# Banks dealt out over the uses that exist, and a new order of tasks on all engines, in a two-layer transformer kernel

## Chip, cores, metric

The kernel runs on one core of one Trainium2 chip. The metric is the device time of one launch in microseconds; lower is better. The whole input of 16 sequences is one launch.

## What is computed

Each of 16 sequences has 512 tokens of 128 features (float32). Two layers follow one another, and in each the attention and the feed-forward network both read the same normalised input and are added to the residual:

```python
xn = _layernorm(x)
x = x + _L0_attn_ref(xn, ...) + _L0_ffn_ref(xn, ...)
xn = _layernorm(x)
x = x + _L1_attn_ref(xn, ...) + _L1_ffn_ref(xn, ...)
```

Layer 0's attention has 16 heads of 64 features, a causal mask and a distance penalty per head. Layer 1's is a differential attention without a mask: 8 heads, each with two softmaxes over 8-feature queries and keys with rotary positions; the second result, times a learned factor, is taken from the first, and each head is normalised before the output projection. Each feed-forward network normalises once more, widens to 512, applies silu and narrows to 128.

## The kernel before

**Sequences and ticks.** Every engine runs a program written out in full, without a loop on the chip. Time is counted in ticks, of which each sequence has a clock of its own. A new sequence starts every 32 ticks (`TICKS`), so that in the middle one period of 32 ticks holds layer 0 of one sequence and most of layer 1 of the one before. Constants such as `FA_AT = 11` or `WOB_AT = 44` (lines 96 to 139) give the tick, on the sequence's clock, at which a task is issued; a tick from 32 on falls in the next period (44 is tick 12 there), a negative one in the period before. `pipeline` (line 563) calls each engine's `body(b)` for b from -1 to 17, and a body goes through ticks 0 to 31. An engine takes its work strictly in this order; engines meet only at semaphores.

**Layer 0** takes two heads (a pair) every four ticks; r is the tick's place in the four. For a pair TensorE projects q and k (r = 0) and v (r = 2), computes scores (`max_scores0`, line 1380: rows 0 and 1 of 128 queries at r = 0, row 2 at r = 1, row 3 at r = 3). VectorE adds the mask and takes the row maximum (`row_max0`), ScalarE exponentiates (`exp0`), VectorE inverts the sums (`invert_sums`), GpSimd scales (`scale_probs`), TensorE transposes in three groups (`turn_probs`, line 1399), ScalarE copies them (`copy_turned`) and TensorE multiplies by v (`pv0`). The output projection comes in two halves, woA and woB (`attention_out`, line 1428). Hidden tiles ya0 to ya3 (layer 1: yb0 to yb3) and the second product fa (fb) are the feed-forward network.

**Layer 1** runs in 46 steps over 28 ticks from tick 58 (`l1_chunk`, line 152), one or two steps in a tick, called its part 0 and part 1. A step has two score tiles for row maxima (`mx1`, steps 0 to 31), and from step 14 on two tiles of transposed scores (`st1`) that ScalarE exponentiates; every second step has a product with the values (`pv1`, line 1442). Both row and key tiles are issued by `second_scores` (line 1469), small transposes by `second_turns` (line 1457), everything that comes once in a sequence by `others`. Queries and keys are rotated on VectorE (`rotate`, line 1104), stored in parts by SyncE's queue (`store_parts`, line 609) and loaded back into the operands QS and KS (`stack`, line 622).

**PSUM banks.** Two banks, `pj`, take all projections and products (63 uses a period); five, `sc`, take score tiles and transposes (224 a period); one, `op`, the layer-1 values. A use's bank is its place in a list of all tasks of a period, modulo two or five: `pj_order` and `score_order` (lines 205 and 243) write that list, and `pj_use` and `tile_before` (lines 339 and 353) tell which use had the bank before, so what an engine must wait for. The place counts all tasks of a full period, also in the first and last periods, where many of them do not run:

```python
def tile_bank(kind, m):

    return TILE_AT[kind, m] % SCB
```

TensorE waits before it writes a bank (`bank`, line 1314, and `bank_free`, line 1369) until VectorE or ScalarE has read the use before.

**Order within a tick.** It is written by hand in each engine's `body`: TensorE's from line 1555, VectorE's from line 1252, ScalarE's from line 931, GpSimd's from line 744, SyncE's from line 641. The tables in the section on the change give it.

## Time and profile before

| what | value |
|---|---|
| time before, median of 3 runs | 2718.11 us (2716.66 to 2722.74) |
| profiled execution, its own time | 2727.31 us |
| its span, first to last instruction | 2725.5 us |
| TensorE busy | 2468.1 us |
| ScalarE / VectorE busy | 1896.9 / 1869.4 us |
| GpSimd busy | 1411.5 us |
| mean granted TensorE clock | 0.982 |

All parts of the prediction rest on one profiled execution, with times in us from the start of its span. TensorE's row of matmuls counts an instruction as busy to a modelled end, so neighbours overlap a little; an idle time in brackets names the instruction on another engine that ended it. A full period is 162.3 us long and repeats to 0.1 us: the input of the next sequence is fetched every 162.30 us.

### The profile page before, as it was taken

How to read it: one execution, taken by the hardware profiler on the slowest of the kernel's cores; microseconds unless marked ns; L12 is line 12 of the kernel's file. 1: busy time of each engine (PE TensorE's matmuls, PEld its weight loads, DVE VectorE, ACT ScalarE, POOL GpSimd, SP SyncE). 2: the span in 40 equal slices, each digit the busy share in tenths (PEclk: the TensorE clock that was granted, in tenths of full speed). 3: DMA queues.
4: the chain of work that ended last, by engine and by line, in shares of the span. 5: the costliest groups of instructions: out<-in, count | busy, mean ns of one | idle time of the engine just before them, and what ended most of it. 6: DMA issues, size and time to landing. Idle time of an engine off the chain costs nothing.

```text
span 2725.5 us, 52475 instructions
## 1 busy us (share of the span) xinstructions
PE 2468.1 (91%) x18176; PEld 1232.3 (45%) x18176; DVE 1869.4 (69%) x5637; ACT 1896.9 (70%) x4707; POOL 1411.5 (52%) x1353
## 2 busy tenths in 40 slices
PE   6899999999999999999999999999999999999877
PEld 3454444454444445444444444445444444544421
DVE  4447677776767767677676867777676776866665
ACT  3766786767777776776767678677777777677435
POOL 4666465554646455464554547455464645546111
PEclk8999999999999999999999999999999999999978
DMA  2002020110202001020200202001020200202020
GB/s 88 5 5 48 5 52 2 31 26 6 51 6 47 5 16 41 6 52 2 49 9 5 52 5 52 2 22 35 6 51 2 52 5 6 51 2 51 2 51 5
DMA packets 59830, 68.57 MB, mean 25 GB/s; under 512 B 11056, under 2 KB 55344, under 8 KB 56368
## 3 DMA queue, kind: packets, MB, share of 16 engines
q1 hardware_dynamic: 59568, 65.21, 10.0%
q8 instruction: 148, 2.42, 0.4%
q14 instruction: 114, 0.93, 0.1%
HBM read 35.04 MB, written 29.36 MB: 24 GB/s over the span
## 4 chain that ended last, share of the span: by engine, by line
PE 65%; DVE 14%; ACT 9%; issue 3%; DMA 0%; SPq 0%; POOLq 0%; DVEq 0%; ACTq 0%; POOL 0%
PE pj L1332 16%; PE sc L1394 10%; PE pj L1424 9%; PE op L1448 8%; PE sc L1492 5%; DVE pq L1095 5%; PE pj L1350 4%; PE pj L1438 4%; ACT pt L885 4%; PE sc L1411 4%; PE sc L1485 3%; DVE mx L1148 2%; PE pj L1324 2%; ACT pt L863 1%; ACT pq L845 1%
## 5 line engine op out<-in xcount | busy, mean ns | idle before, releaser
L713 POOL TENSOR_SCALAR pq<-pq,rsum 128x128 f32<-128x128 f32 (+3 forms) x1024 | 1113.3, 1103 | 1071.3 <-DVE rsum L1102 1071.3
L1148 DVE TENSOR_REDUCE mx<-sc 128x1 f32<-128x512 f32 x1024 | 653.3, 684 | 334.3 <-PE sc L1492 331.3
L885 ACT ACTIVATE pt<-sc 128x512 f32<-128x512 f32 x1024 | 558.4, 608 | 220.2 <-PE sc L1485 219.7
L1095 DVE CUSTOM_DVE_ANT_0 pq<-sc,relkey 128x128 f32<-128x128 f32 (+3 forms) x1024 | 459.0, 486 | 315.5 <-PE sc L1394 308.3
L845 ACT ACTIVATE pq<-pq,mx 128x128 f32<-128x128 f32 (+3 forms) x1024 | 568.0, 568 | 48.6 <-DVE mx L1095 47.3
L863 ACT ACTIVATE pt<-sc 128x512 f32<-128x512 f32 (+1 forms) x768 | 353.8, 530 | 186.9 <-PE sc L1411 185.9
L1394 PE MATMUL sc<-K,Q 64*128 64x128 f32 (+3 forms) x2048 | 383.0, 471 | 25.0 <-ACT pt L885 11.2
L1424 PE MATMUL pj<-pt,v 128*64 128x512 f32 (+3 forms) x2048 | 305.2, 440 | 14.4 <-ACT y L813 8.8
L1332 PE MATMUL pj<-xnT,wqkv 128*128 128x512 f32 x512 | 288.6, 656 | 11.2 <-DVE xb L1069 6.2
L1411 PE MATMUL sc<-ident,pq 64*128 64x64 f32 x5120 | 233.6, 228 | 69.0 <-DVE mx L1095 58.4
L1448 PE MATMUL op<-pt,v 128*32 128x512 f32 x2048 | 279.2, 618 | 13.3 <-ACT pt L885 12.9
L1492 PE MATMUL sc<-KS,QS 48*128 48x512 bf16 x1024 | 243.7, 387 | 47.5 <-DVE mx L1095 20.4
L1411 PEld LDWEIGHTS sc<-ident,pq 64*128 64x128 f32 x5120 | 201.0, 140 | 177.4 <-issue 134.2
L1394 PEld LDWEIGHTS sc<-K,Q 64*128 64x128 f32 x2048 | 147.0, 187 | 252.3 <-issue 158.2
L1485 PE MATMUL sc<-QS,KS 51*128 51x512 bf16 x1024 | 217.2, 387 | 15.8 <-ACT pt L885 10.2
L1424 PEld LDWEIGHTS pj<-pt,v 128*64 128x64 f32 x2048 | 143.0, 137 | 180.0 <-issue 147.8
L845 ACT ACTIVATION_READ_ACCUMULATOR pq<-pq,mx 128x1 f32 x1024 | 210.7, 206 | 0.0
L1485 PEld LDWEIGHTS sc<-QS,KS 51*128 51x128 bf16 x1024 | 54.7, 94 | 222.3 <-issue 134.0
L1492 PEld LDWEIGHTS sc<-KS,QS 48*128 48x128 bf16 x1024 | 60.8, 94 | 196.3 <-DVE mx L1095 64.7
L1332 PE MATMUL pj<-wqkv,xnT 128*128 128x128 f32 x1024 | 147.4, 287 | 1.1 <-DVE K L1076 0.8
L1332 PEld LDWEIGHTS pj<-wqkv,xnT 128*128 128x128 f32 x1024 | 125.8, 193 | 39.7 <-issue 25.7
L811 ACT ACTIVATE tanh<-pj,b1h 128x512 f32<-128x512 f32 x128 | 88.3, 690 | 75.4 <-PE pj L1332 70.4
(105 smaller groups left out, 2822.6 us busy)
## 6 DMA issues: line engine op xcount, KB each, us to landing
scr_p<-y SPq DMA_DIRECT2D x160, 128.0 KB, 2.9
QS<-scr_p SPq DMA_DIRECT2D x32, 384.0 KB, 5.6
KS<-scr_p SPq DMA_DIRECT2D x32, 384.0 KB, 5.6
x_in<-in_L_attn_x SPq DMA_DIRECT2D x16, 256.0 KB, 2.8
scr_p<-tanh SPq DMA_DIRECT2D x32, 128.0 KB, 2.5
out_x<-xres SPq DMA_DIRECT2D x16, 256.0 KB, 2.3
QS<-nrow SPq DMA_DIRECT2D x192, 4.0 KB
wqkv<-in_L_attn_w_qkv SPq DMA_DIRECT2D x1, 1536.0 KB, 6.5
```

The source lines that it names most:

```text
L713: pool.tensor_scalar(rows, rows, rsum[:, p % NROWS, c:c + 1], None, ALU.mult).then_inc(s_scl, 1)
L845: act.activation(rows, rows, ACT.Exp, scale=-1.0, bias=mx0[:, p % NROWS, c:c + 1], accum_out=lsum[:, p % NROWS, c:c + 1]).then_inc(s_exp0, 1)
L863: act.activation(to[:, :, h, :], sc[tile_bank("tr0", m)][:, 0:cols].rearrange("p (n c) -> p n c", c=HALF), ACT.Copy).then_inc(s_ev, 1)
L885: act.activation(pt1[:, GS * (m % 2) + 2 * j + h, :], sc[tile_bank("st1", 2 * n + h)][:, :], ACT.Exp, scale=float(DS) ** -0.25).then_inc(s ...
L1095: dve.tensor_tensor_reduce(out=pq[:, at:at + width], in0=sc[tile_bank("mx0", m)][:, left:left + width], in1=relkey[:, T - width:T], scale= ...
L1148: dve.reduce_max(mx1[:, g % 2, at:at + 1], sc[tile_bank("mx1", 2 * t + h)][:, :], AXIS.X).then_inc(s_mxd1, 1)
L1332: last = pe.matmul(t[:, c * k:c * (k + 1)], w(k), x(k), start=True, stop=True)
L1394: last = pe.matmul(sc[tile_bank("mx0", m + j)][:, left:left + width], Q0[r, b, P * row:P * (row + 1)], K0[r, b, 0:width], start=True, stop ...
L1411: last = pe.transpose(sc[tile_bank("tr0", m + h)][:, HALF * n:HALF * (n + 1)], pq[r, at:at + P], ident[r, r])
L1424: last = pe.matmul(t[DH * j:DH * (j + 1), P * k:T], v0[:, p % NBUF, k, DH * j:DH * (j + 1)], pt[:, base:base + WIDTH[k]], start=k == 0, st ...
L1448: last = pe.matmul(op[32 * j:32 * (j + 1), :], v1[:, k, (GS * g + j) // 2, :], pt1[:, GS * (k % 2) + j, :], start=k == 0, stop=k == NT - 1)
L1492: pe.matmul(sc[tile_bank("mx1", 2 * t + h)][:, :], QS[r, slot, P * q:P * (q + 1)], KS[r, slot, :], start=True, stop=True).then_inc(s_mxf1, 1)
```

## The change

Three things, on all engines together.

1. The lists of bank uses are made over the whole program. `pj_order` and `score_order` now go through all ticks of all sequences, hold only the tasks that run, and `in_turn` deals the banks out one after the other, anew at each period. `tile_before` and `pj_use` look the use up. The two clocks g and h (for tasks of the first and of the second layer) are equal in every tick here, since `CLOCKS` has one entry.
2. Ticks of single tasks move, as the first part of the diff shows; `SCALE_LAG` and `NORM_LAG` move two steps of the head normalisation back in steps of layer 1. `second_scores` is split into `second_keys` (st1) and `second_tops` (mx1), always called in this order.
3. The order within a tick changes. "L1 rows", "L1 scores", "L1 values", "L1" stand for the layer-1 parts; 0 and 1 is the part; "turn 1" is the second group of probability transposes; scores 0, 2, 3 and maxima are by row group:

| engine, r | before | after |
|---|---|---|
| TensorE 0 | q, scores L1 0, k, scores 0, values 0, turn 1, turn 2, rows 0 1, others, values 1, scores L1 1 | q, scores L1 0, rows 0, k, scores 0, turn 1, values 0 1, others, turn 2, rows 1, scores L1 1 |
| TensorE 1 | rows 0, pv, scores L1 0 1, others, values 0, rows 1, scores 2, values 1 | rows 0, pv, scores L1 0, values 0, others, scores L1 1, rows 1, scores 2, values 1 |
| TensorE 2 | scores L1 0, rows 0, v, scores L1 1, others, rows 1, values 0 1 | rows 0, scores L1 0, v, scores L1 1, values 0, others, rows 1, scores 3, values 1 |
| TensorE 3 | rows 0, scores 3, rows 1, scores L1 0, others, values 0, turn 0, values 1, scores L1 1 | rows 0 1, scores L1 0, values 0, others, turn 0, values 1, scores L1 1 |
| VectorE 0 | others, L1 0, maxima 0, norms, copy K, maxima 1, L1 1, invert 2 | invert 1, others, invert 2, L1 0, norms, copy K, maxima 0, maxima 1, L1 1 |
| VectorE 1 | invert 3, L1 0, others, L1 1, norms | invert 3, norms, L1 0 1, others |
| VectorE 2 | norms, others, invert 0, maxima 2, L1 0 1 | maxima 2, norms, others, L1 0, invert 0, L1 1 |
| VectorE 3 | norms, others, maxima 3, L1 0 1, invert 1 | norms, maxima 3, L1 0, others, L1 1 |
| ScalarE 0 | copy Q, L1 0, exp 3, exp 0, others, copy turned 2 3 4, L1 1 | L1 0, exp 3, copy Q, copy turned 2 3, others, copy turned 4 5, L1 1, exp 0 |
| ScalarE 1 | copy turned 5, L1 0, copy attention, others, L1 1, exp 1 | L1 0, others, copy attention, L1 1 |
| ScalarE 2 | L1 0, others, copy v, L1 1 | L1 0, exp 1, L1 1, copy v, others |
| ScalarE 3 | exp 2, others, L1 0, copy turned 0 1, L1 1 | exp 2, L1 0, others, copy turned 0 1, L1 1 |
| GpSimd | r 1: scale 2, small, scale 3; r 2: scale 0, small; r 3: small, scale 1 | r 0: scale 1, small; r 2: scale 2 3 0, small; r 1 and 3: small |

SyncE's queue keeps its order in a tick; the constants move both fills (`STACK_AT`) behind both stores (`STORE_AT`). The diff, cut to the constants, the numbering and TensorE's first tick of four:

```diff
@@ -93,47 +93,48 @@
-X_AT = -18
-LN0_AT = (-14, -9, -1)
+X_AT = -19
+LN0_AT = (-15, -8, -1)
 XNT0_AT = -5
 HT0_AT = -1
-FFN0_AT = (1, 2, 5, 5)
+FFN0_AT = (1, 2, 6, 7)
 FA_AT = 11
 WOA_AT = 35
-WOB_AT = 44
-LN1_AT = (45, 48, 54)
+WOB_AT = 45
+LN1_AT = (47, 48, 54)
 XNT1_AT = 49
 ROPE_AT = (51, 52)
-STORE_AT = (47, 50)
-STACK_AT = (47, 50)
-VALS_AT = 55
+STORE_AT = (49, 50)
+STACK_AT = (54, 54)
+VALS_AT = 54
 HT1_AT = 55
 L1_AT = 58
 L1_TICKS = 28
-FFN1_AT = (56, 56, 57, 59)
+FFN1_AT = (56, 56, 59, 60)
 FB_AT = 62
 TAIL_AT = 86
-TURN3_AT = 86
-OT_AT = 89
-OUT_AT = 90
-HID0_AT = (3, 6, 7, 11)
-HID1_AT = (57, 58, 59, 60)
-ADDA_AT = 12
-ADDB_AT = 63
-ADDWA_AT = 36
+TURN3_AT = 87
+OT_AT = 90
+OUT_AT = 91
+HID0_AT = (2, 5, 7, 10)
+HID1_AT = (57, 59, 60, 61)
+ADDA_AT = 11
+ADDB_AT = 64
+ADDWA_AT = 35
 ADDWB_AT = 45
 TURN_ROPE_AT = (52, 53)
 HEAD3A_AT = 87
-HEAD3B_AT = 90
+HEAD3B_AT = 89
 ADDOUT_AT = 91
-PLN0_AT = (-11, -5)
-PLN1_AT = (48, 49)
-RES0_AT = 3
-RES1_AT = 51
+PLN0_AT = (-9, -7)
+PLN1_AT = (47, 48)
+RES0_AT = 0
+RES1_AT = 53
 HEAD3P_AT = 87
-STOREOUT_AT = 84
+STOREOUT_AT = 89
+CLOCKS = (TICKS * NB,)
...
-SCALE_LAG = 0
-NORM_LAG = 4
+SCALE_LAG = 3
+NORM_LAG = 5
...
+def clocks():
+
+    shown = [(n, n) for n in range(-TICKS, CLOCKS[0])]
+    g = h = CLOCKS[0]
+    for first, second in CLOCKS[1:]:
+        for n in range(max(first, second)):
+            shown.append((g + n if n < first else None, h + n if n < second else None))
+        g, h = g + first, h + second
+    end = TICKS * (NB + 2)
+    while h < end:
+        shown.append((g if g < end else None, h))
+        g, h = g + 1, h + 1
+    return shown
 
 
...
+def in_turn(order, banks):
+
+
+    uses, of_bank, n = {}, [[] for _ in range(banks)], 0
+    for use in order:
+        if use is None:
+            n = 0
+            continue
+        of_bank[n % banks].append(use)
+        uses[use] = (n % banks, len(of_bank[n % banks]))
+        n += 1
+    return uses, of_bank
+
+
 PJ_ORDER = pj_order()
-PJ_AT = {name: n for n, (name, _) in enumerate(PJ_ORDER)}
-PJ_PER = [len(PJ_ORDER[b::2]) for b in range(2)]
-TILES = score_order()
-TILE_AT = {(kind, m): n for n, (kind, _, m) in enumerate(TILES)}
...
+PJ_USES, _ = in_turn(PJ_ORDER, 2)
+TILES, TILES_OF = in_turn(score_order(), SCB)
...
 def tile_before(seq, kind, m):
 
-    n = TILE_AT[kind, m]
-    body = seq.ago(-TILES[n][1])
-    while body.lo >= -1:
-        n -= SCB
-        if n < 0:
-            body = body.ago(1)
-            n = n % SCB + SCB * ((len(TILES) - 1 - n % SCB) // SCB)
-        kind, ago, m = TILES[n]
-        if body.ago(ago).live():
-            return kind, body.ago(ago), m
-    return None
+    bank, n = TILES[kind, m, seq.lo]
+    if n == 1:
+        return None
+    kind, m, lo = TILES_OF[bank][n - 2]
+    return kind, Seq(lo), m
...
-            def body(b):
-
-                used.clear()
-                for n in range(TICKS):
-                    s, r = divmod(n, 4)
-                    if r == 0:
-                        p, i = b.pair(s, -1)
-                        if i is not None:
-                            project_q(i, p)
-                        second_scores(b, n, 0)
-                        p, i = b.pair(s, -1)
-                        if i is not None:
-                            project_k(i, p)
-                        p, i = b.pair(s, 0)
-                        if i is not None:
-                            max_scores0(i, p, 0)
-                        second_values(b, n, 0)
-                        p, i = b.pair(s, 2)
-                        if i is not None:
-                            turn_probs(i, p, 1)
-                        p, i = b.pair(s, 2)
-                        if i is not None:
-                            turn_probs(i, p, 2)
-                        second_turns(b, n, 0)
-                        second_turns(b, n, 1)
-                        others(b, n)
-                        second_values(b, n, 1)
-                        second_scores(b, n, 1)
...
+            def tick(g, h):
+
+                r = (h if g is None else g) % 4
+                if r == 0:
+                    p, i = pair(g, -1)
+                    if i is not None:
+                        project_q(i, p)
+                    second_keys(h, 0)
+                    second_tops(h, 0)
+                    second_turns(h, 0)
+                    p, i = pair(g, -1)
+                    if i is not None:
+                        project_k(i, p)
+                    p, i = pair(g, 0)
+                    if i is not None:
+                        max_scores0(i, p, 0)
+                    p, i = pair(g, 2)
+                    if i is not None:
+                        turn_probs(i, p, 1)
+                    second_values(h, 0)
+                    second_values(h, 1)
+                    others(g, h)
+                    p, i = pair(g, 2)
+                    if i is not None:
+                        turn_probs(i, p, 2)
+                    second_turns(h, 1)
+                    second_keys(h, 1)
+                    second_tops(h, 1)
...
+            pipeline(tick)
+            assert used == [use for use in PJ_ORDER if use is not None]
```

## Rows read from the trace of the kernel before

**Rows 1.** The page, parts 1 and 5: busy time by engine, and one group.

```profile
PE 2468.1 (91%) x18176; PEld 1232.3 (45%) x18176; DVE 1869.4 (69%) x5637; ACT 1896.9 (70%) x4707; POOL 1411.5 (52%) x1353
...
L1148 DVE TENSOR_REDUCE mx<-sc 128x1 f32<-128x512 f32 x1024 | 653.3, 684 | 334.3 <-PE sc L1492 331.3
```

**Rows 2.** Stretches: length, busy us (instructions) by engine, granted clock, DMA share, GB/s.

```profile
71.00:178.00 107.00, 94.07 (x753) 55.12 (x753) 44.90 (x201) 76.81 (x211) 73.74 (x70) 0.97 0.01 4
178.00:326.00 148.00, 135.42 (x1005) 71.13 (x1004) 102.08 (x317) 101.25 (x259) 80.42 (x77) 0.99 0.11 25
...
703.00:865.30 162.30, 150.93 (x1139) 75.90 (x1137) 116.51 (x352) 118.10 (x295) 87.78 (x85) 1.00 0.10 24
...
2654.00:2692.00 38.00, 31.30 (x147) 6.26 (x146) 27.81 (x53) 20.52 (x41) 1.83 (x2) 0.76 0.01 2
```

**Rows 3.** Timeline, TensorE, one period: start, length, line, operation, wait before.

```profile
705.85 0.66 PE L1324 MATMUL pj<-ident,oraw 128*128 128x128 f32 x4 [0.72 <-ACT oraw L869]
...
713.44 0.47 PE L1411 MATMUL sc<-ident,pq 64*128 64x64 f32 x8 [0.44 <-DVE mx L1095]
...
716.41 2.37 PE L1424 MATMUL pj<-pt,v 128*64 128x512 f32 x16 [0.59 <-ACT y L813]
...
720.97 0.38 PE L1492 MATMUL sc<-KS,QS 48*128 48x512 bf16 x2
...
745.88 1.12 PE L1332 MATMUL pj<-xnT,wqkv 128*128 128x512 f32 x2
...
748.80 0.46 PE L1411 MATMUL sc<-ident,pq 64*128 64x64 f32 x8 [0.44 <-DVE mx L1095]
...
776.57 1.12 PE L1332 MATMUL pj<-hT,w 128*128 128x512 f32 x2 [0.45 <-ACT att L836]
...
785.05 0.39 PE L1492 MATMUL sc<-KS,QS 48*128 48x512 bf16 x1 [0.36 <-DVE mx L1095]
785.70 0.71 PE L1411 MATMUL sc<-ident,pq 64*128 64x64 f32 x16 [0.27 <-DVE mx L1095]
...
797.10 0.39 PE L1485 MATMUL sc<-QS,KS 51*128 51x512 bf16 x1 [0.31 <-ACT pt L885]
...
800.48 0.39 PE L1492 MATMUL sc<-KS,QS 48*128 48x512 bf16 x1 [0.23 <-DVE mx L1095]
...
813.18 1.13 PE L1332 MATMUL pj<-xnT,wqkv 128*128 128x512 f32 x2 [0.44 <-DVE xb L1069]
...
825.26 0.92 PE L1394 MATMUL sc<-K,Q 64*128 64x384 f32 x4 [0.56 <-ACT pt L885]
...
826.77 0.63 PE L1324 MATMUL pj<-ident,oraw 128*128 128x128 f32 x4 [0.38 <-DVE xacc L1069]
...
846.68 1.06 PE L1448 MATMUL op<-pt,v 128*32 128x512 f32 x8 [0.32 <-ACT pt L885]
...
857.55 0.46 PE L1411 MATMUL sc<-ident,pq 64*128 64x64 f32 x8 [1.03 <-DVE mx L1095]
...
860.59 2.37 PE L1424 MATMUL pj<-pt,v 128*64 128x512 f32 x16 [0.35 <-DVE y L1116]
```

**Rows 4.** Timeline, VectorE, ticks 31 and 0.

```profile
741.91 0.69 DVE L1069 TENSOR_TENSOR xres<-pj,xacc 128x512 f32<-128x512 f32 x1 [0.73 <-PE pj L1350]
...
748.01 0.29 DVE L1095 CUSTOM_DVE_ANT_0 pq<-sc,relkey 128x128 f32<-128x128 f32 x1 [0.73 <-PE sc L1394]
...
748.57 0.69 DVE L1076 COPY K<-pj 128x512 f32<-128x512 f32 x1
```

**Rows 5.** Timeline, ScalarE, tick 1.

```profile
752.60 0.60 ACT L836 ACTIVATE att<-pj 128x512 f32<-128x512 f32 x1 [1.63 <-PE pj L1424]
754.19 0.69 ACT L811 ACTIVATE tanh<-pj,b1h 128x512 f32<-128x512 f32 x1 [0.99 <-PE pj L1332]
```

**Rows 6.** Timeline, SyncE's queue: stores of key parts, fill of KS.

```profile
702.16 3.15 SPq L620 DMA_DIRECT2D scr_p<-y  x5
...
709.91 0.83 SPq L632 DMA_DIRECT2D KS<-scr_p  x2
```

More of the change, by code:

```diff
@@ new lines, with __init__, upto, ago @@
+class Seq:
+    def __init__(self, lo):
+        self.lo = lo
+    def upto(self, per, n):
+        return self.lo * per + n
+    def ago(self, d):
+        return Seq(self.lo - d)
+    def first(self):
+        return self.lo == 0
+    def live(self):
+        return 0 <= self.lo < NB
+def at(clock, tick):
+    if clock is None or (clock - tick) % TICKS:
+        return None
+    seq = Seq((clock - tick) // TICKS)
+    return seq if seq.live() else None
+def pair(g, lag):
+    if g is None:
+        return 0, None
+    n, p = divmod(g // 4 - lag, NPAIR)
+    return p, Seq(n) if Seq(n).live() else None
@@ new lines, in pairs, with misc @@
+    def pairs(name, g, lag):
+        p, i = pair(g, lag)
+        if i is not None:
+            order.append((f"{name}{p}", i.lo))
+    def misc(g, h):
+        for clock, tasks in ((g, FIRST_MISC), (h, SECOND_MISC)):
+            order.extend((name, i.lo) for tick, name in tasks if (i := at(clock, tick)) is not None)
+    for g, h in clocks():
+        if g is not None and g % TICKS == 0:
+            order.append(None)
+        r = (h if g is None else g) % 4
+        if r == 0:
+            pairs("q", g, -1)
+            second(h, 0)
+            pairs("k", g, -1)
+            misc(g, h)
+            second(h, 1)
@@ new lines, in second_tops, with tops, turned @@
+    def second_tops(h, part):
+        if (i := l1(h)) is not None:
+            for t in l1_chunk(h, part):
+                if t < NU:
+                    order.extend(("mx1", 2 * t + n, i.lo) for n in range(2))
+    def tops(g, lag, q):
+        p, i = pair(g, lag)
+        if i is not None:
+            order.extend(("mx0", 6 * p + max(0, 2 * (q - 1)) + j, i.lo) for j in range(2))
+    def turned(g, lag, group):
+        p, i = pair(g, lag)
+        if i is not None:
+            order.extend(("tr0", 6 * p + 2 * group + n, i.lo) for n in range(2))
@@ L774, in _ @@
+            pipeline(tick)
         @block.scalar
```

779 lines of the change are left out of this document (370 added, 409 removed).

## Prediction

> **What bounds the kernel now.** First the page's table of busy time: TensorE is busy 91% of the span, ScalarE 70%, VectorE 69%, GpSimd 52% [rows 1]. So the kernel is nearly all TensorE's work, and what the other engines can cost is the time in which TensorE stands still. Then the table of stretches: a full sequence takes 162.3 us and TensorE is busy 150.93 of them, idle 11.37; thirteen such periods lie between 326 and 2436 us. The first two sequences (107 and 148 us) and the end, where the last sequence's layer 1 runs alone, are emptier: of 38 us near the end TensorE is busy 31.30 [rows 2].
>
> Third, TensorE's timeline over one period. The bracket behind an instruction says how long TensorE stood before it, and for whom. There are 25 such waits, 10.8 us together, of 0.2 to 1.0 us each; those that matter here are shown [rows 3]. None is for a transfer and none for GpSimd. Nearly all are one pattern: TensorE wants a PSUM bank that VectorE or ScalarE has not read yet, because too little TensorE work lies between two uses of it. So the order of the tasks, not the amount of work, is what can still be gained or lost.
>
> **What the change does.** No operation is added, removed or resized. Three things move: (a) a PSUM bank is given out over the tiles that really run, not by a fixed place in the period; (b) the ticks of single tasks; (c) the order inside a tick, on all engines.
>
> (a) In the middle every tile runs, so the round is the same: 224 tiles in five banks, begun anew each period. Counted from the lists of tasks, the old numbering brings a bank back after only 1 or 2 tiles 21 times in the first sequence and 24 times in the second, and after 3 tiles 38 times in the last stretch; the new one always waits for five. It can act in the thin parts only. The first two sequences stand 12.9 and 12.6 us [rows 2], some 3 us above two full periods, and I take that: -3 (bounds 0 and -6). In the 38 us near the end 6.7 are idle, and I put half down to the banks: -3 (bounds 0 and -7).
>
> (b) and (c) in the middle, wait by wait [rows 3]. Ticks count 0 to 31; tick 24 begins at 709.7, tick 0 at 744.5, tick 12 at 811.1, tick 20 at 851.5 us.
> - 705.85 (0.72): the last transpose of heads followed straight on the copy of them. It moves from tick 86 to 87, behind some 1.6 us of work. Gone.
> - 713.44 (0.44), and the same at 731.14 and 816.09: the third group of probability transposes needs the bank of the row-0 scores. It now stands behind `others` and the layer-1 values, so in ticks 24, 28 and 12 there come 1 to 2 us between. Gone, 1.31 in all. In ticks 0 and 8 nothing comes between: 748.80 and its like stay.
> - 716.41 (0.59): the same move puts 0.4 us between hidden tile yb0 and its bank's next use. 0.4 gone.
> - 776.57 (0.45): ya2 and ya3 leave tick 5 for 6 and 7. Gone. 785.05 and 785.70 (0.36, 0.27): the row-3 scores come earlier and over 1 us goes between. Gone. 800.48 (0.23): the small transpose goes between, 0.2 gone.
> - 813.18 (0.44): the add that empties fa's bank runs in tick 11, not 12. Gone.
> - 825.26 and 826.77 (0.56, 0.38): woB moves to tick 13, between the layer-1 tiles and the row-2 scores. Both gone.
> - 846.68 (0.32): row-3 scores go ahead of the values. Gone.
>
> Sum: 0.72 + 1.31 + 0.4 + 0.45 + 0.63 + 0.2 + 0.44 + 0.94 + 0.32 = 5.4 us. Not gained: 857.55 and 860.59 (1.03, 0.35). The transposes there move behind rk and rks, but both waits hang on VectorE's seven steps of rotation, and the next bank, whose reader now stands behind layer-1 work on VectorE, is late instead. I count 0 (bounds -1.0 and +1.0).
>
> New waits, bounded by their neighbours. First, the add behind fb goes from tick 63 to 64, behind the row-3 maxima and two layer-1 maxima of 0.68 us. Now it starts right behind the matmuls, at 741.91; there it would end some 4.3 us behind them [rows 1, 4], and k wants the bank about 4.0 us behind them: 0.3 us. Second, ScalarE now takes `others` before the copy of attention. In tick 1 that copy, now free at 753.2, goes behind tanh and y of ya0, whose tanh starts at 754.19 [rows 5]: done at about 755.7, where v wants the bank at some 755.3: 0.4 us. Third, woB no longer covers the copy of the third group in tick 12: 0.3 us. Together 1.0.
>
> Net -4.4 by this list. But a removed wait lets TensorE reach the next bank sooner, and twice the list shows this at once: 797.10 (0.31) goes while the row-2 scores behind it lose their cover, and the rotation above. From below nothing survives (0), from above all of it (-4.4). I take -2.7 a period, nearer to the list since its waits lie in different parts of the period: 13 x -2.7 = -35 us.
>
> Transfers: the stores of key parts (702.16) no longer queue behind the fill of QS, and both fills now come behind all stores. In the middle 11 us lie between the issue of KS at 709.91 [rows 6] and its first user at 720.97 [rows 3], and the stores come 2 us sooner, which covers the order. At the end the same stores stand in the chain: -2 (bounds 0 and -3). GpSimd's scalings move behind other small work; it is busy 52% and no wait of the period is for it, so I cost it at nothing; without that cover a probability transpose would wait about 1 us a pair.
>
> Sum: -35 - 3 - 3 - 2 = -43 us on the profiled execution's own 2727.3, so 2684. That execution lies 9.2 us above the median of 2718.1; the same change put there gives **2675**. (0.2%, or 5.4 us, is about what a measurement of this kernel can tell from no change.)
>
> A busy row can hide waiting. Where a wait cuts a pair of layer-1 tiles in two (785.05), the second takes 0.39 us alone. The Trainium skill, "Trainium Kernel Development and Optimization", Performance Expectations, says that matmul busy time is a bad measure of how close a kernel is to its limit, because matmuls are pipelined. By that page more than 11.37 us a period is there to be won, which is on the next rival's side.
>
> **Rivals.** *More* (2653): the whole list survives, 13 x -4.4 = -57, with the ends -65. For it: each wait was costed where it stands, and no engine but TensorE is busy over 73% of a period. Against: the two places where a wait only moves. In the 38 us near the end the granted clock is 0.76 against 1.00 in the middle [rows 2], so part of it ran at 1.2 GHz and not 2.4. The Trainium skill, "TensorE: Matmul & The Clock Gate", Part 1, calls the throttled state the default that activity releases. By that page closing gaps there gives some more, which the sum leaves out.
>
> *Less* (2703): waits are passed on to the next bank; -0.5 a period, so -7, and -8 from the ends. For it: TensorE takes its work in order, and 748.80 shows what an uncovered place costs. Against: the covers of (b) are 1 us and more.
>
> *Slower* (2746): VectorE's copy of K now stands before the row-0 maxima. In tick 0, K's bank is full at about 747.0 (the row at 745.88 of [rows 3]) and VectorE is free from 747.3, since it is idle 0.73 us before the maxima at 748.01 [rows 4]. The copy (0.69 us, now at 748.57) just fits in and costs nothing. If VectorE comes to it later, each of the eight pairs loses up to 0.69 us before its third transposes, 5.5 us a period. It decides from 3.3 us a period on, five pairs of eight wholly exposed: then -2.7 and the ends are eaten. All of it: (5.5 - 2.7) x 13 = +36, ends -8, +28. Against: VectorE is idle 0.25 to 2.5 us before these maxima in seven of the eight pairs.
>
> *Nothing* (2718): the new numbering changes nothing in the middle, and the moved tasks hide what they hid before.
>
> **How the numbers follow.** Forecast 0.45, more 0.23, less 0.17, slower 0.10, nothing 0.05. The range goes from 2643 (more, and a little from the clock) to 2710 (beyond less); it leaves out slower, nothing and the edges of the others, about 0.2. Faster by over 0.2%: forecast, more and nearly all of less, 0.84. Within: nothing and the rest, 0.06. Slower: 0.10.
>
> **What would show it.** A period of 159.6 us, not 162.3, with TensorE still busy some 150.5. No wait for oraw before the last heads, none for xb or xacc; third-group transposes waiting in ticks 0, 8 and 20 only; new short waits for att in tick 1 and for xres behind fb. Mean times of one instruction stay. It is wrong if the period stays or grows, and the rival on K is right if the transposes' wait in ticks 0 and 8 rises from 0.44 towards 1.1 us.

## The result: 115 us less, and the profile after

The changed kernel takes **2603.64 us** (2599.53 to 2608.86, 4 runs) beside 2718.87 for the kernel before: ratio **0.9576, 95% interval 0.9555 to 0.9597**, faster by 115 us. The profiled execution has a span of 2603.2 us. The page, parts 1 and 5 (against [rows 1]):

```profile
PE 2442.8 (94%) x18176; PEld 1234.9 (47%) x18176; DVE 1853.8 (71%) x5637; ACT 1886.7 (72%) x4707; POOL 1414.8 (54%) x1353
...
L1165 DVE TENSOR_REDUCE mx<-sc 128x1 f32<-128x512 f32 x1024 | 654.6, 682 | 213.4 <-PE sc L1514 212.2
```

The same instructions run, with the same mean times (this group 682 ns, 684 before). TensorE is busy 94% of a shorter span. A stretch of one period in the middle, in the columns of [rows 2]:

```profile
612.47:767.21 154.74, 149.72 (x1137) 75.94 (x1136) 114.98 (x352) 117.50 (x295) 88.08 (x85) 1.00 0.11 25
```

Against the 162.30 and 150.93 us of [rows 2], 7.5 us of a period are gone: TensorE's idle time fell from 11.37 to 5.0 us, and its busy time, with the same instructions, by 1.2 us. Busy ends are modelled in this profile, so the 1.2 us is the less certain of the two. A period here and in all that follows is taken between starts of the matmuls of fa, whose tick 11 did not move: from the third sequence's (318.09 before, 302.90 after) to the sixteenth's (2428.53, 2315.50), by 13. That gives 162.34 before and **154.82** after.

TensorE's timeline over that period, all waits of 0.2 us and more. There were 25 before, 10.8 us in all, part of them in [rows 3]; there are 12 now, 4.7 us:

```profile
664.40 2.37 PE L1440 MATMUL pj<-pt,v 128*64 128x512 f32 x16 [0.34 <-ACT pt L883]
...
675.16 1.98 PE L1348 MATMUL pj<-xnT,wqkv 128*128 128x512 f32 x4 [0.39 <-ACT xnT L813]
...
681.00 2.37 PE L1440 MATMUL pj<-pt,v 128*64 128x512 f32 x16 [0.20 <-ACT y L833]
...
699.32 0.92 PE L1410 MATMUL sc<-K,Q 64*128 64x384 f32 x4 [0.66 <-DVE mx L1165]
...
713.48 0.46 PE L1427 MATMUL sc<-ident,pq 64*128 64x64 f32 x8 [0.44 <-DVE mx L1112]
...
720.00 1.16 PE L1348 MATMUL pj<-wqkv,xnT 128*128 128x128 f32 x8 [0.35 <-ACT att L856]
...
723.87 0.39 PE L1514 MATMUL sc<-KS,QS 48*128 48x512 bf16 x1 [0.36 <-DVE mx L1112]
...
729.44 0.39 PE L1514 MATMUL sc<-KS,QS 48*128 48x512 bf16 x1 [0.35 <-ACT pt L883]
...
741.66 0.39 PE L1514 MATMUL sc<-KS,QS 48*128 48x512 bf16 x1 [0.22 <-DVE mx L1112]
...
755.05 0.47 PE L1427 MATMUL sc<-ident,pq 64*128 64x64 f32 x8 [0.44 <-DVE mx L1112]
...
761.04 0.92 PE L1410 MATMUL sc<-K,Q 64*128 64x384 f32 x4 [0.56 <-ACT pt L905]
...
766.90 0.39 PE L1514 MATMUL sc<-KS,QS 48*128 48x512 bf16 x1 [0.36 <-DVE mx L1112]
```

Nothing is left ahead of 664.40, from tick 11 on, where the kernel before had seven waits up to and with the same task (813.18 to 860.59 in [rows 3]). The third groups of transposes wait in ticks 0 and 8 only (713.48, 755.05), still 0.44 us each. The longest wait of before, 1.03 us at 857.55 of [rows 3], which the prediction had left standing, is gone too.

Over the whole, 13 x 7.52 = 98 us of the 115 lie in the middle and 17 in the first sequences and the tail.

### The profile page after: what moved, and what is told of

Same layout as the page of the kernel before. It is cut to its first block, busy times and chain, and to the rows that moved or that the text cites. A ratio compares the mean times of both kernels' runs of the same rounds, so it can differ in the third digit from the quotient of the medians.

```text
span 2603.2 us, 52473 instructions
## 1 busy us (share of the span) xinstructions
PE 2442.8 (94%) x18176; PEld 1234.9 (47%) x18176; DVE 1853.8 (71%) x5637; ACT 1886.7 (72%) x4707; POOL 1414.8 (54%) x1353
## 3 DMA queue, kind: packets, MB, share of 16 engines
q8 instruction: 148, 2.42, 0.4%
## 4 chain that ended last, share of the span: by engine, by line
PE 80%; DVE 8%; ACT 7%; issue 3%; POOL 0%; DMA 0%; SPq 0%; POOLq 0%; DVEq 0%; ACTq 0%
PE pj L1348 21%; PE sc L1410 11%; PE pj L1440 11%; PE op L1464 8%; PE sc L1427 6%; PE sc L1497 5%; PE pj L1366 5%; PE sc L1514 5%; PE pj L1454 5%; DVE pq L1112 3%; DVE mx L1165 2%; PE pj L1340 2%; ACT pt L905 2%; ACT pt L883 1%; ACT pq L865 1%
## 5 line engine op out<-in xcount | busy, mean ns | idle before, releaser
L1112 DVE CUSTOM_DVE_ANT_0 pq<-sc,relkey 128x128 f32<-128x128 f32 (+3 forms) x1024 | 450.8, 487 | 222.2 <-PE sc L1410 216.0
L1348 PE MATMUL pj<-xnT,wqkv 128*128 128x512 f32 x512 | 282.1, 642 | 11.6 <-ACT xnT L813 5.5
L1514 PE MATMUL sc<-KS,QS 48*128 48x512 bf16 x1024 | 252.0, 389 | 32.9 <-DVE mx L1112 14.2
L865 ACT ACTIVATION_READ_ACCUMULATOR pq<-pq,mx 128x1 f32 x1024 | 217.4, 212 | 0.0
L1497 PE MATMUL sc<-QS,KS 51*128 51x512 bf16 x1024 | 204.2, 388 | 3.6 <-ACT pt L905 1.8
L1366 PE MATMUL pj<-w,y 128*128 128x128 f32 x1024 | 129.9, 288 | 4.0 <-DVE y L1081 4.0
```

Source lines behind the costliest of these rows:

```text
L865: act.activation(rows, rows, ACT.Exp, scale=-1.0, bias=mx0[:, p % NROWS, c:c + 1], accum_out=lsum[:, p % NROWS, c:c + 1]).then_inc(s_exp0, 1)
L1112: dve.tensor_tensor_reduce(out=pq[:, at:at + width], in0=sc[tile_bank(i, "mx0", m)][:, left:left + width], in1=relkey[:, T - width:T], sca ...
L1348: last = pe.matmul(t[:, c * k:c * (k + 1)], w(k), x(k), start=True, stop=True)
L1497: pe.matmul(sc[tile_bank(i, "st1", 2 * m + n)][:, :], KS[r, slot, P * k:P * (k + 1)], QS[r, slot, :], start=True, stop=True).then_inc(s_st ...
L1514: pe.matmul(sc[tile_bank(i, "mx1", 2 * t + n)][:, :], QS[r, slot, P * q:P * (q + 1)], KS[r, slot, :], start=True, stop=True).then_inc(s_mx ...
```

## Experiments

All are timed against the kernel before on the same chip. The first table is what they come to; "period" and "idle" (TensorE's, from stretches of nine periods) are each read from one profiled execution, in us. The row of the changed kernel is there to compare with.

| run | ratio (95%) | us | period | idle |
|---|---|---|---|---|
| before | 1 | 2719 | 162.34 | 11.37 |
| changed | 0.9576 (0.9555 to 0.9597) | 2604 | 154.82 | 5.10 |
| banks_only | 0.9966 (0.9954 to 0.9979) | 2710 | 162.37 | 11.38 |
| old_banks | 0.9617 (0.9603 to 0.9632) | 2616 | 154.79 | 5.04 |
| group3_alone | 0.9918 (0.9892 to 0.9945) | 2695 | 160.91 | 9.84 |
| tensor_new_alone | 0.9872 (0.9848 to 0.9896) | 2685 | 161.07 | 10.00 |
| small_adds | 0.9928 (0.9902 to 0.9954) | 2700 | 160.67 | 9.98 |
| before_res1_50 | 0.9997 (0.9989 to 1.0006) | 2721 | 162.34 | 11.37 |
| old_tensor_order | 0.9823 (0.9809 to 0.9838) | 2672 | 159.43 | 9.29 |
| group3_back | 0.9863 (0.9850 to 0.9877) | 2683 | 160.68 | 10.76 |
| group3_k_back | 0.9777 (0.9756 to 0.9798) | 2659 | 159.14 | 9.22 |
| old_scalar_order | 1.0066 (1.0044 to 1.0088) | 2737 | 164.62 | 11.49 |
| old_gpsimd_order | 0.9537 (0.9512 to 0.9562) | 2593 | 154.37 | 4.71 |
| unlisted_ticks_back | 0.9668 (0.9649 to 0.9686) | 2629 | 157.51 | 7.58 |
| wob_tick44 | 0.9641 (0.9628 to 0.9654) | 2623 | 156.40 | 6.56 |
| res1_tick51 | 0.9519 (0.9504 to 0.9533) | 2589 | 154.37 | 4.70 |
| res1_51_att_first | **0.9485** (0.9472 to 0.9498) | **2581** | 153.95 | 4.35 |
| k_behind_maxima | 0.9643 (0.9621 to 0.9665) | 2623 | 157.18 | 6.01 |

In four of these the mean hides two kinds of periods, those at the full granted clock and some in which it fell for a few us: without a fall a period takes 160.27 in group3_back (10 of 13), 158.71 in group3_k_back (11), 160.80 in tensor_new_alone (11) and 163.0 in old_scalar_order (5). VectorE's order was not undone as a whole in any run, only its copy of K, and the order of the transfers in none.

### The bank numbering alone, and undone

banks_only is the kernel before with this (in short, not the code):

```
 # order and ticks of before
-bank = place of the use in the period % banks
+bank = count of the uses that exist, begun anew each period, % banks   (in_turn)
```

> The order and the ticks of before, the banks dealt over the uses that exist. The prediction's theory: it acts in the thin parts only, so the middle period stays 162.3 us to 0.05, and the whole gives -6 us (-3 in the first two sequences, -3 in the tail), 0.998. Rival 1 (the numbering is what made the head and the tail gain more than I said): -15 to -24 us, 0.991 to 0.994, with the first three first-layer hidden-by-output matmuls (fa) 7, 6 and 2 us earlier. Rival 2 (the numbering does nothing, the order did it all): within 2 us of before. Now that I have seen the changed kernel's head, where waits for row maxima fell by a few us only, I lean to -6.

old_banks is the changed kernel with dead uses counted again:

```
         if use is None: n = 0; continue
+        if not use: n += 1; continue      # a use that does not exist keeps its place
```

> The new order and ticks, but a bank by its fixed place in the period, as before. Period in the middle 154.8 us, as with the new banks. Prediction's theory: the whole is 6 us slower than the changed kernel (about 2610, 0.960). Rival 1: 15 to 24 us slower (0.963 to 0.967). Rival 2: no difference.

The middle does not move (162.37 and 154.79). Alone the numbering is worth 9 us (6 to 13 by its interval), undone it costs 11 (0.9617 against 0.9576; the two intervals lie 0.0006 apart, so this size is loose). It acts in the thin parts only, as predicted. Its size lies between the forecast's 6 us, which the first interval just holds, and the 15 of the first rival.

### TensorE's order, the third group, and K's copy

old_tensor_order is the changed kernel with TensorE's order in all four kinds of tick (and the order in which banks are dealt) as before; the first of the four:

```
 r == 0: q, keys, tops,
-        turns, k, max0, turn 1, values, values, others, turn 2, turns, keys, tops
+        k, max0, values, turn 1, turn 2, turns, turns, others, values, keys, tops
```

> The changed kernel with only TensorE's order inside a tick (and with it the order in which banks are dealt) put back; ticks and the other engines' orders stay new. If the waits that I put down to TensorE's order are what went (turn group 3: 1.31; hidden yb0 .4; .63 around the row-3 scores; .2; .32; and the 1.03 before the transposes of tick 20), the period rises by 3 to 4 us, from 154.8 to about 158.5, and the whole by some 50 us (0.976). Rival: the ticks carry the gain (oraw .72, woB .94, xb .44, ya2 .45): then the period rises by under 1.5 us (0.965 or less). A second rival: old TensorE order against new orders of the readers is worse than both, over 162.3.

group3_back moves one task of the changed kernel:

```
                     turn_probs(i, p, 1)
+                    turn_probs(i, p, 2)
                     second_values(h, 0)
                     second_values(h, 1)
                     others(g, h)
-                    turn_probs(i, p, 2)
```

> The changed kernel with only the third group of probability transposes put back right behind the second on TensorE. My prediction's term for this was 1.31 us a period, with 0.4 at hidden yb0 beside it and nothing for the wait of 1.03 in tick 20. Theory now: this one move carries most of TensorE's order: +1.3 (term alone) to +3 us a period with tick 20's, 156 to 158 us, whole +20 to +40 us (0.965 to 0.972). Rival: the gain sits in the other moves of TensorE's order (row-3 scores and keys), so under +0.7 us.

The one move costs 5.9 us a period (5.5 without the falls of the clock), far above both expectations and above undoing the whole order (4.6). Its long waits on TensorE's timeline, in ticks 12, 20, 24 and 28:

```profile
641.18 0.47 PE L1427 MATMUL sc<-ident,pq 64*128 64x64 f32 x8 [0.89 <-DVE mx L1112]
...
681.26 0.47 PE L1427 MATMUL sc<-ident,pq 64*128 64x64 f32 x8 [1.80 <-DVE mx L1112]
...
700.33 0.46 PE L1427 MATMUL sc<-ident,pq 64*128 64x64 f32 x8 [1.35 <-DVE mx L1112]
...
717.47 0.46 PE L1427 MATMUL sc<-ident,pq 64*128 64x64 f32 x8 [0.80 <-DVE mx L1112]
```

The same places cost 0.43, 1.03, 0.44 and 0.44 before. In old_tensor_order they cost 0.89, nothing, 1.35 and 0.79, so the difference between the two runs is tick 20. There `values` stands ahead of these transposes in old_tensor_order, and GpSimd's adds start only 0.27 us after VectorE's last step of rotation has begun, which takes 0.69 us; in group3_back they run into it, and it takes 1.66:

```profile
675.95 0.69 DVE L1145 TENSOR_TENSOR tanh<-y 128x512 bf16<-128x512 f32 x1
676.22 1.57 POOL L720 TENSOR_TENSOR xacc<-xacc,xn 128x512 f32<-128x512 f32 x1
```

```profile
678.24 1.66 DVE L1145 TENSOR_TENSOR tanh<-y 128x512 bf16<-128x512 f32 x1
678.05 1.30 POOL L720 TENSOR_TENSOR xacc<-xacc,xn 128x512 f32<-128x512 f32 x1
```

So something else in the change makes these waits longer, and the new place on TensorE hides them. group3_k_back tests K's copy on VectorE, by putting it back as well:

```
-                    copy_k(i, p)
                     row_max0(i, p, 0)
+                    copy_k(i, p)
                     row_max0(i, p, 1)
```

> The changed kernel with the third group put back (as in group3_back, 160.68 us a period, waits of 0.89, 1.80, 1.35, 0.80 and four of 0.44 before it) and also VectorE's copy of K put back between the two pairs of row-0 maxima. Theory (the prediction's slower rival, its price being real but covered): the long waits fall by up to 0.7 us each towards 0.44, in three or four pairs, and the period by 2 to 2.5 us, to 158.2 to 158.7 (0.971 to 0.974). Rival: K's place does not matter, the waits come from the second-layer work ahead on VectorE: period stays 160.7 within 0.3.

Ticks 12 and 28 fall to 0.44 us, and tick 20 to 1.21: K's new place is the whole excess of two of these waits and 0.6 us of a third. The period falls by 1.5 us, less than expected, since in tick 20 the last step of rotation still takes 1.66 us, and tick 24 now waits for ScalarE:

```profile
670.07 0.47 PE L1427 MATMUL sc<-ident,pq 64*128 64x64 f32 x8 [1.21 <-DVE mx L1112]
...
688.54 0.46 PE L1427 MATMUL sc<-ident,pq 64*128 64x64 f32 x8 [0.75 <-ACT pt L883]
```

group3_alone makes the move in the kernel before, and tensor_new_alone all of TensorE's new order (with the new banks):

```
 # group3_alone, kernel before, r == 0
-                            turn_probs(i, p, 2)
                         second_turns(b, n, 0)
                         second_turns(b, n, 1)
                         others(b, n)
+                            turn_probs(i, p, 2)
```

> The kernel before with one move: the third group of probability transposes goes behind turns and others on TensorE, in every fourth tick; banks, ticks and the other engines' orders stay. Prediction's term: 1.31 us a period (ticks 24, 28, 12). Theory now: it takes the waits of ticks 12, 20, 24 and 28, 0.43 + 1.03 + 0.44 + 0.44 = 2.3 us, and with each wait some 0.1 us of busy time: period about 159.7, whole -35 us (0.987). In the changed kernel the same move undone cost 5.9 us a period; if it is worth as much here (period 156.5, 0.972), the new order of VectorE has no part in that price.

> The kernel before with all of TensorE's new order inside a tick and the new banks; ticks and the orders of VectorE, ScalarE and GpSimd stay old. Beside it the run with the new banks alone (162.37 us a period). Theory now: the orders need each other. The waits of ticks 12, 24 and 28 go (1.3), that of tick 20 mostly moves to the next bank as in group3_alone, and the period comes to 160 to 161 us (0.982 to 0.988). Rival: TensorE's order is worth here what it was worth undone in the changed kernel, 4.6 us: 157.8 us (0.970).

Alone they bring 1.4 and 1.3 us a period (1.4 and 1.5 without falls of the clock). The waits of ticks 12 and 24 go, that of tick 28 stays at 0.44. That of 1.03 us in tick 20 is passed on, first to the bank of rk (a second-layer key projection), held by the copy of K behind the rotation, then to pv: 0.49 + 0.80 us in group3_alone, 0.60 + 0.80 in tensor_new_alone, where 1.03 + 0.35 stood. group3_alone:

```profile
684.34 1.12 PE L1332 MATMUL pj<-xnT,w_l 128*128 128x512 f32 x2 [0.49 <-DVE K L1076]
686.88 2.37 PE L1424 MATMUL pj<-pt,v 128*64 128x512 f32 x16 [0.80 <-DVE y L1116]
```

That is just what the prediction said of this place, but in the full change 0.34 us is left of it. Which part does this was not isolated. One part is seen in the section on GpSimd: in tensor_new_alone two steps of the rotation take 1.39 and 1.64 us beside GpSimd's adds, in the changed kernel only the last one is long.

### ScalarE's order

```
 # old_scalar_order: changed kernel, ScalarE's ticks as before (r == 0 and 1 left out here)
 r == 2: second_attention,
-        exp0(1), second_attention, values, others
+        others, values, second_attention
 r == 3: exp0(2),
-        second_attention, others, turned(0), turned(1), second_attention
+        others, second_attention, turned(0), turned(1), second_attention
```

> The changed kernel with ScalarE's old order inside a tick. Prediction: the wait of 0.35 us for att in tick 1 goes (the copy of attention stands ahead of others again), nothing else changes: 154.4 us, 0.955. Theory now: the new order also brings the first exponentials of a pair behind the copies of turned probabilities, and without it the third group or pv waits for ScalarE: 155 to 157 us, 0.960 to 0.970.

A miss by far: 9.8 us a period, and slower than before. `others` holds the tanh of a hidden part. ya2 and ya3 are in ticks 6 and 7 now, and TensorE issues them behind the tick's layer-1 tiles. ScalarE in its old order comes to the tanh first and stands there, with the copy of v and the exponentials of those tiles queued behind, and TensorE wants the banks of these exponentials next. ScalarE, then TensorE, ticks 6 and 7:

```profile
772.49 0.69 ACT L831 ACTIVATE tanh<-pj,b1h 128x512 f32<-128x512 f32 x1 [2.31 <-PE pj L1348]
773.07 0.68 ACT L833 ACTIVATE y<-pj,b 128x512 f32<-128x512 f32 x1
773.64 0.60 ACT L850 ACTIVATE v<-pj 128x512 f32<-128x512 f32 x1
```

```profile
774.87 1.13 PE L1410 MATMUL sc<-K,Q 64*128 64x512 f32 x4 [2.42 <-ACT pt L905]
...
780.53 0.71 PE L1427 MATMUL sc<-ident,pq 64*128 64x64 f32 x16 [1.94 <-ACT pt L905]
```

These two waits are 4.4 us of the 8.2 that a period without a fall of the clock loses (162.99 against 154.8); the falls make it 9.8 in the mean. In tensor_new_alone, which has the same old order on ScalarE but ya2 and ya3 in tick 5, the same two places cost 0.67 and 0.56 us. So the ticks of ya2 and ya3 and the place of `others` on ScalarE belong together; this is read from the waits, and no run undoes the two together.

### GpSimd beside VectorE

The kernel before, tick 19: two steps of VectorE's first rotation, and GpSimd's two residual adds beside them.

```profile
851.77 1.54 DVE L1120 TENSOR_TENSOR y<-y 128x512 f32<-128x512 f32 x1
853.34 1.38 DVE L1122 CAST y<-y 128x512 bf16<-128x512 f32 x1
854.76 0.74 DVE L1124 TENSOR_TENSOR y<-y 128x512 f32<-128x512 f32 x1
```

```profile
851.49 1.27 POOL L697 TENSOR_TENSOR xacc<-xacc,xn 128x512 f32<-128x512 f32 x1
852.84 1.60 POOL L701 TENSOR_TENSOR xacc<-xacc,bias 128x512 f32<-128x512 f32 x1
```

before_res1_50 is the kernel before with `RES1_AT = 50` for 51.

> The kernel before with one constant changed: GpSimd's two residual adds go from tick 51 to 50, out of VectorE's first rotation. Theory (GpSimd's adds slow the VectorE steps that run beside them): the rotation's steps of 1.54 and 1.38 us fall to about 0.7 and 0.43, TensorE's wait of 1.03 us before the transposes of tick 20 goes or falls below 0.3, and the period comes to 161.3 us or so, the whole to -10 to -15 us (0.995). Rival (those steps are long for another reason, or the wait is passed on): period 162.3 as before.

Nothing moved, the adds neither: GpSimd is behind its ticks there and runs them right behind its reciprocal root in any case (that ends and the adds begin at the same place of the period). The run says nothing on the theory. small_adds cuts the adds themselves, so its kernel leaves out most of the second layer's residual and bias:

```
-pool.tensor_tensor(xacc[:, :, :], xacc[:, :, :], xn[:, :, :], ALU.add)
+pool.tensor_tensor(xacc[:, :, 0:1], xacc[:, :, 0:1], xn[:, :, 0:1], ALU.add)
 # and the same for the bias
```

> The kernel before, with GpSimd's two residual adds of the second layer cut from 512 columns to 4 (every 128th): the rest of the residual and of the bias is left out. Nothing else changes. Theory (GpSimd's work slows the VectorE steps that run beside it): rotation steps of 1.54 and 1.38 us fall towards 0.7 and 0.43, the maxima come 1 to 1.7 us sooner, TensorE's 1.03 us before the transposes of tick 20 shrink to 0.44 or less and the whole by 6 to 13 us (0.995 to 0.998). Rival 1: GpSimd's next scalings just move into their place and slow the same steps: steps 1 us or more still. Rival 2: the steps get short but another wait takes over: period 162.3.

```profile
680.31 0.69 DVE L1120 TENSOR_TENSOR y<-y 128x512 f32<-128x512 f32 x1
681.04 0.45 DVE L1122 CAST y<-y 128x512 bf16<-128x512 f32 x1
681.52 0.69 DVE L1124 TENSOR_TENSOR y<-y 128x512 f32<-128x512 f32 x1
```

The steps fall from 1.54 and 1.38 to 0.69 and 0.45 us, both waits of tick 20 (1.03 and 0.35) are gone and the period is 1.7 us shorter. GpSimd's adds cost TensorE 1.7 us a period without TensorE ever waiting for GpSimd. The Trainium skill, "SBUF — State Buffer", SBUF: two separate sides, says that GpSimd shares a pair of ports with those VectorE instructions that run in a two-port mode or have two inputs from SBUF, and that whichever starts first holds it for its whole instruction, while the other is blocked. By that rule the first step, which has two such inputs, should stand until the add ends; the trace agrees: the add ends at 852.76, the step at 853.31. It does not agree for every GpSimd instruction: in the changed kernel GpSimd's reciprocal root, whose inputs are in SBUF too, runs beside four of the steps, and they take 0.69, 0.43, 0.69 and 0.43 us (two are shown):

```profile
656.94 2.38 POOL L744 TENSOR_TENSOR rms<-mse,minus_half 128x8 f32<-128x8 f32 x1
```

```profile
656.94 0.69 DVE L1137 TENSOR_TENSOR y<-y 128x512 f32<-128x512 f32 x1
657.67 0.43 DVE L1139 CAST y<-y 128x512 bf16<-128x512 f32 x1
```

In the changed kernel the adds are at tick 53. res1_tick51 puts `RES1_AT` back from 53 to 51, old_gpsimd_order GpSimd's order inside a tick (the scalings of one pair spread over ticks again).

> The changed kernel with one constant put back: GpSimd's two adds of the second layer's residual go from tick 53 to 51, beside VectorE's first rotation. In the kernel before, two of the rotation's steps took 1.54 and 1.38 us while those adds ran, against 0.69 and 0.43 in the changed kernel. Theory A (the engines slow each other, and the rotation stands before the row-0 maxima): the steps stretch again, by 1.5 us or so in all, and TensorE waits at the transposes of tick 20 or at the next bank: period +0.3 to +1.0 us, whole +5 to +15 us. Rival B (it stretches, but rk and rks, 2 us of work now ahead of the third group of transposes, cover it): steps longer, period within 0.15 us of 154.8. Rival C: no step gets longer; then the stretch of before had another cause.

> The changed kernel with GpSimd's old order inside a tick. Prediction: nothing, since TensorE waits for GpSimd nowhere in the middle; period 154.8. Theory now: GpSimd also works through VectorE's speed, so what runs beside the rotations matters: the steps stretch in other places, TensorE is mostly covered: 154.5 to 155.3. Rival: over 155.5, then GpSimd's order is one of the sources of the gain.

Both come out *faster* than the changed kernel, by 0.45 us a period (by the whole time, res1_tick51 lies clear of it, 0.9504 to 0.9533 against 0.9555 to 0.9597, and old_gpsimd_order does not). With GpSimd's new order, tick 51 puts the adds ahead of the rotation, and no step of the first rotation is long; at tick 53 they run into its last step, and VectorE comes 1 us later to K and the maxima. In old_gpsimd_order two scalings go ahead of the adds, which fall into the second rotation; there a step takes 1.61 us, and TensorE loses nothing by it. The changed kernel:

```profile
659.13 1.29 POOL L720 TENSOR_TENSOR xacc<-xacc,xn 128x512 f32<-128x512 f32 x1
```

```profile
659.32 1.65 DVE L1145 TENSOR_TENSOR tanh<-y 128x512 bf16<-128x512 f32 x1
```

res1_tick51, the same step:

```profile
654.28 0.69 DVE L1145 TENSOR_TENSOR tanh<-y 128x512 bf16<-128x512 f32 x1
```

TensorE's 0.34 us at 664.40 goes with it, in both runs. Of the three theories rival C had it that no step gets longer, but its conclusion, another cause for the stretch of before, is refuted by small_adds; none had said that the kernel gets faster. By its ratio res1_tick51 gains some 15 us, of which 13 x 0.45 = 6 lie in the middle; the rest was not looked into.

### Ticks

wob_tick44 has `WOB_AT = 44` for 45; unlisted_ticks_back has

```
-X_AT = -19; LN0_AT = (-15, -8, -1); PLN0_AT = (-9, -7); RES0_AT = 0
+X_AT = -18; LN0_AT = (-14, -9, -1); PLN0_AT = (-11, -5); RES0_AT = 3
-VALS_AT = 54; FFN1_AT = (56, 56, 59, 60); HID1_AT = (57, 59, 60, 61); ADDB_AT = 64
+VALS_AT = 55; FFN1_AT = (56, 56, 57, 59); HID1_AT = (57, 58, 59, 60); ADDB_AT = 63
-ADDWA_AT = 35; STORE_AT = (49, 50); STACK_AT = (54, 54); SCALE_LAG = 3; NORM_LAG = 5
+ADDWA_AT = 36; STORE_AT = (47, 50); STACK_AT = (47, 50); SCALE_LAG = 0; NORM_LAG = 4
```

> The changed kernel with the second half of the output projection (woB) put back from tick 45 to 44. Prediction's terms: 0.94 us come back before the row-2 scores and the transposes of heads, 0.3 us of new wait in tick 12 never came, so +0.9 us a period, 155.7 us, whole +13 us (0.962). Rival: with the other tasks where they are now, something else already covers those banks: within 0.3 us.

> The changed kernel with the ticks put back that my list gave no gain: load of x, both steps of the first LayerNorm with GpSimd's part and residual, values of the second layer, hidden yb with its VectorE part, the adds behind fb and woA, the stores and fills, the lags of GpSimd's head scaling and its norm. Prediction: they are worth nothing or little (they took away a new wait of at most 0.3 us): period within 0.3 us of 154.8, whole within 8 us of the changed kernel (0.955 to 0.961). Rival: the part of 7.5 us that neither TensorE's order (4.6) nor woB (1.6) holds is theirs: period +1 us or more, 0.963 or more.

woB's tick is worth 1.6 us a period: the two waits that it covers came back as 0.56 and 0.59, and one of pv behind the rotation grew from 0.34 to 0.73. The ticks that I had priced at nothing are worth 2.7. The third group waits again in ticks 16 and 28, v of tick 26 waits for att, for twice what v of tick 2 does, and the transposes of heads wait for 0.34 us:

```profile
643.50 0.46 PE L1427 MATMUL sc<-ident,pq 64*128 64x64 f32 x8 [0.76 <-DVE mx L1112]
...
686.31 1.16 PE L1348 MATMUL pj<-wqkv,xnT 128*128 128x128 f32 x8 [0.78 <-ACT att L856]
...
697.11 0.47 PE L1427 MATMUL sc<-ident,pq 64*128 64x64 f32 x8 [0.80 <-DVE mx L1112]
```

Tick 28 is plain: yb3 moves from tick 60 to 59 and no longer lies between the groups there. Which constants make the other two was not tried.

### Two tries at a faster version

res1_51_att_first adds to res1_tick51, on ScalarE:

```
 r == 1:
-                    others(g, h)
                     copy_attention(i, p)
+                    others(g, h)
```

> An attempt at a faster version: residual adds back at tick 51, and on ScalarE the copy of attention ahead of others in ticks 1, 5, ... If the 0.35 us of TensorE's wait for att in tick 1 is due to that order, as the prediction had it, it goes: period 154.4 - 0.4 = 154.0 us, whole 2583 us (0.950). Rival: another user of ScalarE (tanh, so y and pv) is then late by as much: 154.4 as in the run before.

As expected: the wait of 0.35 us for att goes and no other comes. At 0.9485 it is the fastest version, some 25 us under the changed kernel by the two ratios.

k_behind_maxima goes on from there:

```
 # TensorE, r == 0
-                    project_k(i, p)
                     max_scores0(i, p, 0)
+                    project_k(i, p)
 # VectorE: copy_k behind both row_max0
```

> A try at a faster version, on top of the last one (153.95 us a period): on TensorE the row-0 scores go ahead of the projection k, which then lies between them and the transposes (1.06 us), and on VectorE the copy of K goes behind both pairs of maxima. If the two waits of 0.44 us left in ticks 0 and 8 are for want of work between, they go: period 153.95 - 0.88 - 0.2 = 152.9 us, whole 2567 us (0.944). Rival: K's bank, freed 0.7 us later, holds the next transposes or projections, and it comes out at 154 or more.

It loses 3.2 us a period. The two 0.44s go, but TensorE now comes to the row-0 scores 1.1 us earlier and waits there for ScalarE, in four pairs of eight; two of them:

```profile
618.97 0.93 PE L1410 MATMUL sc<-K,Q 64*128 64x128 f32 x8 [0.56 <-ACT pt L905]
...
639.72 0.93 PE L1410 MATMUL sc<-K,Q 64*128 64x128 f32 x8 [0.25 <-ACT pt L905]
```

Its idle time rises by 1.7 us only; TensorE's busy time rises by 1.5 (149.60 to 151.15) with the same instructions. Why is open.

## Why the prediction was right in its sign and wrong in its size

**What bounds the kernel**: right in the main. 6.3 of the 7.5 us a period are idle time of TensorE, nearly all of it waits for banks; no wait for GpSimd or a transfer came or went in the middle. The other 1.2 us are busy time.

**(a) Numbering**: right in place, and -6 (bounds 0 to -13) against -9 alone and 11 undone. (That the new numbering "always waits for five" is not quite so: begun anew each period, it comes back after four at the start of one, as the old one did, since 224 is not a multiple of five.)

**The middle**, forecast -2.7 us a period, measured -7.52. The steps that failed, in order of size:
- *"I take -2.7, nearer to the list."* The list's own net was -4.4. The waits on it, 5.4 us, are all gone. The discount of 1.7 us, for waits handed on to the next bank, had hardly a counterpart (797.10, below, is one). 22 us of the whole.
- *"I count 0"* for 857.55 and 860.59, and no term for 749.86, 790.85 and 797.10. The first two went from 1.38 to 0.34 us. The prediction hung them on VectorE's rotation and took its speed as given; small_adds shows that both waits go when GpSimd's adds beside it are cut. In the changed kernel the adds still stretch the last step, and group3_back, with 1.80 us there, shows that the third group's new place is needed too. Of the others, two went and the third became a wait of 0.56 at the row-2 scores. *New waits, 1.0*: the one for att came (0.35 against 0.4), those for xres and in tick 12 did not, and one of 0.39, q of tick 24 for the copy of hT1, I had not seen. In brackets all this makes -6.1, not -4.4: 22 us.
- *"with TensorE still busy some 150.5."* It is busy 149.73, 1.2 us less than before, and the gaps too small for a bracket fell by 0.2: 18 us. The prediction said that a busy row can hide waiting, gave the pair cut in two (0.39 us for the second tile) and left it out of the sum. There are 7 cut pairs a period before and 4 after; at most part of the 1.2 is theirs, for old_tensor_order has 8 and is busy 150.15 only. How busy time hangs on order stays open. That busy time leaves something to be won besides the 11.37 us of idle time, as the prediction concluded from its citation, holds to these 1.2 us; the prediction had no size for it.

These add up: the forecast's 2.7, and 1.7 + 1.7 + 1.2 + 0.2 = 4.8 us that it missed, make 7.5, times 13 is 98.

**Costs put at nothing.** GpSimd: the reason (no wait is for it) was no reason, since it sets VectorE's speed; 1.7 us a period in the kernel before, and 0.45 lost by the change itself. The unlisted ticks: 2.7. ScalarE's order, for which I had only a cost (0.4): 9.8 when undone. These do not add up to 7.5, and the third group alone (priced at 1.31, 5.9 undone, 1.4 done alone) shows why: a part's worth depends on the others. The list priced each move against the old order; several moves earn nothing there and only keep the others' gains.

**The ends**: forecast -8, measured some -17, of which 9 to 11 are the numbering. The rest was not taken apart, and the -2 for the order of the transfers has no run. Two profiled executions do not settle it: the first fa starts at 66.33 us in the kernel before and at 62.22 in before_res1_50, which does the same up to there.

**The rivals.** *More* (2653) had the right reading of the list and still gave only 65 of the 115 us. The gain that it hoped for from the clock at the end did not come: behind the sixteenth fa the mean granted clock is 0.88 before and 0.87 after. *Slower*: K's copy costs nothing where it stands, as the forecast said, and ticks 0 and 8 stay at 0.44. But its price is real: 1.5 us a period as soon as the third group is uncovered, against 5.5 at most by the rival. *Less* and *nothing* are refuted: a period lost 7.5 us, not 0.5 or none.

## What to carry to other kernels

Where several in-order engines pass banks to each other, price a new order as a whole: for each wait ask what would queue ahead of its releaser in the *new* order of every engine, and test parts by undoing them in the new kernel as well as doing them in the old. Do not discount a list of waits that one can name without naming where each would reappear. An engine that nobody waits for can still be dear, if it lengthens the instructions of one that somebody waits for: compare the single times of one step in different periods and places, not the mean.

## What the runs showed of the hardware that I had not expected

- GpSimd's elementwise adds lengthen VectorE's steps beside them from 0.69 to 1.54 and from 0.45 to 1.38 us; its reciprocal root beside the same kinds of steps leaves them at 0.69 and 0.43.
- In old_scalar_order, whose TensorE stands 2.42 and 1.94 us within 8 us, the granted clock falls from 2.4 to 1.2 GHz for some microseconds at or right behind these waits, in most periods of the middle. From the start of the row-3 scores to the end of the projection q (774.87 to 783.77) it takes 8.9 us without a fall, and 13.3 us (937.83 to 951.14) with two of them. The same 14 us of a period with and without:

```profile
937.00:951.00 14.00, 11.23 (x48) 2.76 (x48) 4.59 (x11) 6.77 (x15) 0.00 (x0) 0.63 0.00 0
...
774.00:788.00 14.00, 10.53 (x87) 4.22 (x88) 7.78 (x23) 10.95 (x26) 3.66 (x4) 1.00 0.00 0
```

- Long waits are not needed for a fall, nor enough: tensor_new_alone has one in 2 of 13 periods, behind waits of 0.23 and 0.68 us, group3_back in 3 of 13, there behind its wait of 1.8 us, and the other periods with the same waits keep 2.4 GHz. In the kernels before and after the clock stays at 1.00 in the middle.
- TensorE's busy time (with modelled ends) for one and the same set of matmuls ran from 149.55 (group3_back) to 151.53 us (old_scalar_order) in single periods at the full granted clock, by order and waits alone.
